# Level tables of a pre-LN attention and experts kernel: from 32 small loads per head to whole tables kept in memory

## Chip, cores and metric

The kernel runs on one core of one Trainium2 chip. The metric is the device time of one execution in microseconds (us). The engines are TensorE (PE, with its weight loads as PEld), VectorE (DVE), ScalarE (ACT), GpSimd (POOL) and SyncE (SP). SP computes nothing: it waits for semaphores and issues transfers, in the order of its program.

## The reference, cut to what matters

Eight sequences of 1024 tokens with 128 channels pass a layer of attention with a decay and a layer of eight experts of which two are used. In the attention a score is multiplied by a decay and by a weight that depends on the level of the distance between query and key (level 0 for distance 0, level l for a distance from 2^(l-1) up to 2^l):

```python
b, t, _ = x.shape                                   # 8, 1024, 128; H = 8 heads, LV = 12 levels
q = (x @ Wq.T).reshape(b, t, H, S); k = ...; v = ...
g = -jax.nn.softplus(x @ Wg.T + bg)
lam = jax.nn.softplus((x @ Wdl.T).reshape(b, t, H, LV) + Lparam)
G = jnp.cumsum(g, axis=1)
scores = jnp.einsum('bthd,bshd->bhts', q, k) * scale
decay = exp(G[t] - G[s]) for s <= t, else 0
lamw[b, h, t, s] = lam[b, t, h, level(t - s)]
A = scores * decay * lamw
out = einsum(A, v) @ Wo.T + x, then layer norm, then a top-2 mixture of 8 experts
```

## The kernel before

The 64 pairs of sequence and head are numbered n = 8 b + h and are worked through in one pipeline. Keys and queries are cut into tiles of 128. Within a head the scores fall into 12 groups (`GROUPS`), and each engine runs through 48 places (four for each group) in an order written out by hand: tables such as `PE_MORE`, `DVE_MORE` and `ACT_MORE` say which further piece stands at which place of which head. While the scores of head n are made, PE makes the logarithms of the weights of head n + 1 (`unit`, matmuls of line 1549 into `l_ps`), and ACT turns them into weights (`exps`, line 846). The preparation of sequence b + 1 and the end of sequence b - 1 are spread over the eight heads of sequence b.

The level weights come to PE in three tables for each head: `ra` (levels 0 to 7 for the query's own key tile), `rc` (levels 1 to 8 for the tile before) and `rb` (levels 8 to 10 for tiles 2 and 4 back). They are the moving operand; the masks are the stationary one. A table has one row for each offset of a query in a block, level and part (high, low); all of a row is zero (or a fixed number) but the queries of that offset, so that the data lie on a diagonal. The tables have two buffers each, filled with their fixed numbers once at the start. For each head SP loads the diagonal pieces from a scratch in device memory: 8 transfers for `ra`, 8 for `rc` (line 458) and 16 for `rb` (line 471). In the buffers the offset is not the outer index, so that a row's piece lies in runs of eight numbers (16 bytes).

Levels 9 and 10 of the farther keys take another way: rows of `ef_scratch` are spread to all partitions, `far` (line 480) and `farther` (line 485). ACT takes the exponential of `farther` for head n + 1 at place 15 of head n (`farther_exps`, line 863). DVE multiplies the query by it at place 21 (`take_q`, line 1087), then takes the low part of the query (line 1091), which frees a bank of `aux`; PE uses the product much later, for head n + 1 (`state_values`, line 1628).

Once a sequence, at h = 4 in SP's loop, `store_el` stores the logarithms of the next sequence: it waits until DVE has written their low parts (which is at place 243 of the sequence, that is place 3 of head 5), and then issues five stores (lines 451, 452 and 476). Only behind it come, in SP's program, `load_next_farther(n + 2)`, that is `farther` for head 6, and the tables for head 7. The order of SP in one step of its loop is:

```python
if h == 4 and b + 1 < B:
    store_el(b + 1)
if n + 2 < NH:
    load_next_farther(n + 2)
if n + 3 < NH:
    load_levels(n + 3)
```

Of the kernel before, what the change touches and what calls it, by code (L numbers as in the profile page):

```python
# [20 lines left out]
P = 128  # L21
# [55 lines left out]
_at = 0  # L77
for _name, _n in (("ma0", NTA * P), ("ma1", NTA * P), ("mb2", NTB * P), ("mb4", NTB * P),
                  ("ident", P), ("tri", P), ("suf", P), ("first", E), ("off", TA)):
    CONST[_name] = (_at, _at + _n)  # L80
    _at += _n
NCONST = _at
NMASK = CONST["ident"][0]
NCST = NCONST


def constants():

    def level(d):
        return np.where(d <= 0, 0, np.floor(np.log2(np.maximum(d, 1))).astype(np.int64) + 1)  # L90

    out = np.zeros((P, NCONST), np.float32)
    row = np.arange(P)
    s = np.arange(P)[None, None, :]

    def put(name, a):
# [12 lines left out]
    col = np.arange(TA)[None, :]  # L109
    off = np.where(q_a[:, 0] > col, NEVER, np.where(col == TA - 1, PAIR - 2 * PAIR * low_part[:, 0], 0.0))  # L110
    put("off", off * at_zero[:, 0] * (q_a[:, 0] != col))
    put("ma1", level(P + t_a - s) == l_a + 1)
# [12 lines left out]

def program(nc, x, Wq, Wk, Wv, Wg, bg, Wdl, Lparam, Wo, ln_g, ln_b, fWg, fbg, fWe, fbe, masks, table, out):

    m_dram = nc.dram_tensor("m_scratch", [H, P, 2, P], F32, kind="Internal").ap()
    n_dram = nc.dram_tensor("n_scratch", [H // 2, P, 2, 2, P], F32, kind="Internal").ap()
    ea_dram = nc.dram_tensor("ea_scratch", [B, H * (LOW + 1), 2, T], F16, kind="Internal").ap()  # L130
    eb_dram = nc.dram_tensor("eb_scratch", [B, H * HIGH, 2, T], F16, kind="Internal").ap()
    ef_dram = nc.dram_tensor("ef_scratch", [B, HIGH * H + H, NF], F32, kind="Internal").ap()

    with ExitStack() as outer:
        def sb(name, shape, dt=F32):
            return outer.enter_context(nc.sbuf_tensor(name, shape, dt))

        cst = sb("cst", [P, NCST - NMASK])
        mask = sb("mask", [P, NMASK], F16)
# [12 lines left out]

        main_stage(nc, x, Wq, Wk, Wv, Wg, bg, Wdl, Lparam, Wo, ln_g, ln_b, fWg, fbg, fWe, fbe, masks, table, out,
                   m_dram, n_dram, ea_dram, eb_dram, ef_dram, cst, mask, m, c, rows,
                   wet_hi, wet_lo, fwg2, wcat)
# [117 lines left out]
def main_stage(nc, x, Wq, Wk, Wv, Wg, bg, Wdl, Lparam, Wo, ln_g, ln_b, fWg, fbg, fWe, fbe, masks, table, out,  # L273
               m_dram, n_dram, ea_dram, eb_dram, ef_dram, cst, mask, m, c, rows,
               wet_hi, wet_lo, fwg2, wcat):

    with ExitStack() as ctx:
# [12 lines left out]
        nt = sb("nt", [P, 2, 2, P], F32R)  # L290
        ra = [sb(f"ra{k}", [P, NTA, TA, NC], F16) for k in range(2)]
        rc = [sb(f"rc{k}", [P, NTA, TA, NC], F16) for k in range(2)]
        rb = [sb(f"rb{k}", [KB, NTB, TB, NC], F16) for k in range(2)]

# [104 lines left out]
        out_done = [sem(f"out_done{f}") for f in range(2)]  # L399
        RA_IN, RB_IN, EL = TA * 16, TB * 16, 5 * 16  # L400
        lng = rows[:, NLOG:NLOG + P]
# [52 lines left out]
        def load_low(eng, n, qs, tables, first, landed):  # L454
            b, h = divmod(n, H)
            at = h * (LOW + 1) + first
            for q in qs:
                eng.dma_start(tables[n % 2][q * 2 * LOW:(q + 1) * 2 * LOW, :, q, :],  # L458
                              ea_dram[b, at:at + LOW, :, q * T // TA:(q + 1) * T // TA]
                              .rearrange("l r (t i) -> (l r) t i", i=NC)).then_inc(landed[n % 2], 16)  # L460

        def load_ra(eng, n, qs):
# [5 lines left out]
        def load_rb(eng, n, qs):  # L468
            b, h = divmod(n, H)
            for q in qs:  # L470
                eng.dma_start(rb[n % 2][q * 2 * HIGH:(q + 1) * 2 * HIGH, :, q, :],  # L471
                              eb_dram[b, h * HIGH:(h + 1) * HIGH, :, q * T // TB:(q + 1) * T // TB]
                              .rearrange("l r (t i) -> (l r) t i", i=NC)).then_inc(rb_in[n % 2], 16)
# [68 lines left out]
        with nc.Block() as block:  # L542
            @block.sync
            def _(sp):
                def load_x(b):
                    if b:
                        sp.wait_ge(t["stored"], EL * b)
                    sp.dma_start(tx[:, :, :], x[b].rearrange("(i t) c -> t i c", i=NC)).then_inc(t["x_in"], 16)

                def store_el(b):  # L550
# [3 lines left out]
                    sp.wait_ge(t["el_far"], 2 * (b + 1))  # L554
                    for part in range(2):
                        store_el_part(sp, b, part)
                    store_el_far(sp, b)

                def load_levels(n):
                    if n >= 2:  # L560
                        sp.wait_ge(l_mm, NU * (n - 1))
                    sp.wait_ge(t["stored"], EL * (n // H + 1))
# [7 lines left out]
                def load_next_farther(n):  # L570
                    sp.wait_ge(cq_done, n - 1)
                    sp.wait_ge(t["stored"], EL * (n // H + 1))
                    load_farther(sp, n)

                def load_last_x():
                    sp.wait_ge(t["stored"], EL * B)
                    sp.wait_ge(e["xb"], 2 * (B - 1))
# [46 lines left out]
                sp.dma_start(per_head(we), fWe.rearrange("e o c -> o e c")).then_inc(s_we, 16)  # L624
                sp.dma_start(mask[:, :], masks).then_inc(mask_in, 16)
                sp.wait_ge(s_hi, 1)
# [30 lines left out]
                for n in range(NH):  # L657
# [31 lines left out]
            def _(pool):  # L689
# [121 lines left out]
                for k in range(2):  # L811
                    pool.tensor_copy(ra[k][:, :, :, :], c("off")[:, None, :, None].broadcast_to([P, NTA, TA, NC])).then_inc(zeroed, 1)
                pool.wait_ge(ready, 3)
# [19 lines left out]
            def _(act):  # L833
# [75 lines left out]
                def token_abs(b):  # L909
                    if b:  # L910
                        act.wait_ge(t["stored"], EL * b)
                    for f in range(2):
# [611 lines left out]
            def _(pe):  # L1524
# [5 lines left out]
                def unit(n, u):  # L1530
                    k = n % 2
                    if u == 0:
                        pe.wait_ge(ra_in[k], RA_IN * (n // 2 + 1))
                    if u == 1:
                        pe.wait_ge(rc_in[k], RA_IN * (n // 2 + 1))
                    if u == 2:
                        pe.wait_ge(rb_in[k], RB_IN * (n // 2 + 1))
                    if n:
# [14 lines left out]
                    for d, i0, cnt in UNITS[u]:  # L1553
                        l_bank = [l_region(n, u)[:, f, slot * HF:(slot + cnt) * HF].rearrange("p (c i) -> p c i", i=cnt)
                                  for f in range(2)]
                        if d <= 1:
                            for tb in range(NTA):
                                f, at = divmod(tb * TA, HF)
                                last = mm(f, l_bank[f][:, at:at + TA, :], m(f"ma{d}")[:, tb * P:(tb + 1) * P],
                                          (ra, rc)[d][k][:, tb, :, i0:i0 + cnt])  # L1560
                        if d in (2, 4):
                            for tb in range(NTB):
                                f, at = divmod(tb * TB, HF)
                                last = mm(f, l_bank[f][:, at:at + TB, :], m(f"mb{d}", KB)[:, tb * P:(tb + 1) * P],
                                          rb[k][:, tb, :, i0:i0 + cnt])
                        slot += cnt
# [332 lines left out]
```

## Time and profile before

| what | value |
|---|---|
| time, median of 3 runs | 1448.07 us (1447.06 to 1449.88) |
| profiled execution, its own time | 1450.03 us |
| its span in the trace | 1448.2 us |
| PE busy | 1319.1 us, 91% |
| ACT busy | 1113.0 us, 77% |
| DVE busy | 1088.8 us, 75% |
| POOL busy | 798.9 us, 55% |
| packets of transfers | 414492, of which 339336 under 512 B |

A share of busy time says which engine has most to do over the whole run; a wait says who was held, by whom, and for how long. Matmuls are pipelined, so a PE that is busy isn't one at its peak. The profiled execution took 1450.03 us, 1.96 us more than the median.

### The profile page before, as it was taken

To read this page: it belongs to the slowest core of one execution; us is meant where nothing else is said; L and a number is where in the kernel's file an instruction comes from. 1 tells how busy PE (TensorE), PEld (TensorE's weight loads), DVE (VectorE), ACT (ScalarE), POOL (GpSimd) and SP (SyncE) were. 2 spreads that over 40 slices of the span, in tenths; PEclk is the share of its full clock that TensorE was granted. 3 is DMA by queue.
4 is the path that set the end of the run, shared out by engine and by line. 5 is a ranking of instruction groups with operands and counts; after the bars stand their busy time and mean duration, and the time that the engine had idled before them with its cause. 6 is when DMAs were issued, how large, how long until landed. Compare 5 with 4: busy or idle time off the path is not lost.

```text
span 1448.2 us, 31450 instructions
## 1 busy us (share of the span) xinstructions
PE 1319.1 (91%) x10278; PEld 1147.7 (79%) x10278; DVE 1088.8 (75%) x2732; ACT 1113.0 (77%) x3270; POOL 798.9 (55%) x956
## 2 busy tenths in 40 slices
PE   4699899989989899889999899998999989989987
PEld 4488788878888788777888788887888878878874
DVE  4757767787867878678776888678786787768777
ACT  3589888887788778888788877888778876877742
POOL 2244458744585456843568354873458544584553
PEclk9899999999999999999999999999999999999998
DMA  5422233223332243222332223322333223322300
GB/s 175 109 43 49 42 67 71 39 42 57 57 70 43 40 75 54 45 48 42 71 71 48 41 37 72 70 36 42 57 56 71 44 44 60 58 57 29 66 8 15
DMA packets 414492, 80.37 MB, mean 55 GB/s; under 512 B 339336, under 2 KB 404090, under 8 KB 414202
## 3 DMA queue, kind: packets, MB, share of 16 engines
q1 hardware_dynamic: 410984, 77.85, 28.5%
q8 instruction: 83, 1.36, 0.4%
q10 hardware_dynamic: 3346, 0.51, 0.2%
q14 instruction: 79, 0.65, 0.2%
HBM read 67.64 MB, written 10.09 MB: 54 GB/s over the span
## 4 chain that ended last, share of the span: by engine, by line
PE 42%; DVE 16%; ACT 14%; POOL 12%; SPq 7%; issue 5%; DMA 4%; ACTq 0%; POOLq 0%; DVEq 0%
PE o_ps L1606 9%; ACT w_all L846 5%; POOL a_lo_all L694 4%; PE s_ps L1526 4%; PE aux L1526 4%; PE s_ps L1528 4%; PE s_ps L1527 4%; SPq L458 3%; PE l_ps L1549 3%; PE aux L1528 3%; PE aux L1527 3%; DMA late<-in_L_attn_x 3%; SPq L471 2%; DVE a_all L1152 2%; DVE late L1382 2%
## 5 line engine op out<-in xcount | busy, mean ns | idle before, releaser
L694 POOL TENSOR_TENSOR a_lo_all<-a_all,a_hi 128x256 fp32r<-128x256 f32 (+2 forms) x576 | 580.4, 1021 | 545.8 <-ACT a_hi L894 544.9
L1152 DVE TENSOR_TENSOR a_all<-s_ps,w_all 128x512 f32<-128x512 f32 (+3 forms) x768 | 365.0, 485 | 185.5 <-PE s_ps L1528 123.2
L894 ACT ACTIVATE a_hi<-a_all 128x256 fp32r<-128x256 f32 (+2 forms) x576 | 308.1, 543 | 198.5 <-DVE a_all L1152 196.9
L846 ACT ACTIVATE w_all<-l_ps,bias 128x128 f32<-128x128 f32 x1589 | 440.4, 394 | 17.4 <-PE l_ps L1549 15.8
L1606 PE MATMUL o_ps<-a_hi,v_all 128*128 128x256 f32 (+2 forms) x1152 | 407.9, 362 | 4.5 <-POOL a_lo_all L694 4.5
L1606 PEld LDWEIGHTS o_ps<-a_hi,v_all 128*128 128x128 f32 x1152 | 222.3, 193 | 21.5 <-issue 3.9
L1526 PE MATMUL s_ps<-q_hi,xt_hi 128*128 128x256 f32 (+2 forms) x576 | 217.1, 377 | 6.9 <-DVE a_all L1152 5.7
L1528 PE MATMUL s_ps<-q_hi,xt_lo 128*128 128x256 f32 (+2 forms) x576 | 198.3, 344 | 0.0
L1527 PE MATMUL s_ps<-q_lo,xt_hi 128*128 128x256 f32 (+2 forms) x576 | 198.3, 344 | 0.0
L1606 PE MATMUL o_ps<-a_lo_all,v_all 128*128 128x256 f32 (+2 forms) x576 | 196.4, 341 | 0.0
L1526 PEld LDWEIGHTS s_ps<-q_hi,xt_hi 128*128 128x128 f32 x576 | 112.0, 194 | 18.0 <-DVE a_all L1152 9.7
L1382 DVE SCALAR_TENSOR_TENSOR late<-aux,gl,late 128x128 f32<-128x128 f32 x392 | 110.9, 343 | 16.5 <-PE aux L1528 16.5
L1528 PEld LDWEIGHTS s_ps<-q_hi,xt_lo 128*128 128x128 f32 x576 | 111.3, 193 | 8.5
L1527 PEld LDWEIGHTS s_ps<-q_lo,xt_hi 128*128 128x128 f32 x576 | 112.3, 195 | 6.8
L1606 PEld LDWEIGHTS o_ps<-a_lo_all,v_all 128*128 128x128 f32 x576 | 112.1, 195 | 5.7
L1078 DVE CAST q_hi<-aux 128x512 fp32r<-128x512 f32 x128 | 88.1, 688 | 32.9 <-PE aux L1528 31.7
L1121 DVE TENSOR_TENSOR v_all<-aux,v_all 128x512 fp32r<-128x512 f32 x128 | 87.9, 686 | 25.5 <-ACT v_all L886 25.1
L1549 PEld LDWEIGHTS l_ps<-rb,mask 96*128 96x128 f16 x1016 | 43.6, 98 | 74.5 <-issue 70.4
L1526 PE MATMUL aux<-nt,xt_hi 128*128 128x256 f32 x256 | 78.2, 305 | 25.2 <-DVE v_all L1121 20.5
L857 ACT ACTIVATE w_all<-far,bias 128x128 f32<-128x128 f32 x320 | 99.8, 389 | 0.0
L1549 PE MATMUL l_ps<-rb,mask 96*128 96x64 f16 (+1 forms) x1016 | 59.4, 202 | 41.0 <-ACT w_all L846 37.1
L1091 DVE TENSOR_TENSOR q_lo<-aux,q_hi 128x512 fp32r<-128x512 f32 x128 | 88.5, 692 | 4.4
(260 smaller groups left out, 2673.2 us busy)
## 6 DMA issues: line engine op xcount, KB each, us to landing
far<-ef_scratch SPq DMA_DIRECT2D x64, 320.0 KB, 3.6
rb<-eb_scratch SPq DMA_DIRECT2D x1016, 0.8 KB
farther<-ef_scratch SPq DMA_DIRECT2D x64, 192.0 KB, 3.4
ra<-ea_scratch SPq DMA_DIRECT2D x508, 4.0 KB, 2.2
rc<-ea_scratch SPq DMA_DIRECT2D x508, 4.0 KB, 2.0
mt<-m_scratch SPq DMA_DIRECT2D x62, 128.0 KB, 3.5
nt<-n_scratch SPq DMA_DIRECT2D x62, 128.0 KB, 3.4
tx<-in_L_attn_x SPq DMA_DIRECT2D x9, 512.0 KB, 5.6
```

The costliest lines, as they stand in the source:

```text
L694: pool.tensor_tensor(a_lo[r][:, 0:t1 - t0], a[r][:, 0:t1 - t0], a_hi[r][:, 0:t1 - t0].bitcast(F32), ALU.subtract).then_inc(a_lo_done, 1)
L846: last = act.activation(w[k][:, W_AT[j] + d, :].rearrange("p (f c) -> p f c", f=2), l_tiles[:, :, :, i - i0], ACT.Exp, bias=bias[b % 2][:, ...
L857: last = act.activation(w[k][:, W_AT[j] + FAR0, :], far[k][:, j * P:(j + 1) * P], ACT.Exp, bias=bias[b % 2][:, h, BIAS_AT[FAR0] + j:BIAS_A ...
L894: act.activation(a_hi[r][:, 0:t1 - t0], a[r][:, 0:t1 - t0], ACT.Copy).then_inc(a_hi_done, 1)
L1091: dve.tensor_tensor(q_lo[n % 2][:, cols], bank(piece), q_hi[n % 2][:, cols].bitcast(F32), ALU.subtract).then_inc(freed(piece), 1)
L1152: dve.tensor_tensor(a[(n * NG + g) % NA][:, 0:t1 - t0], s_ps[:, g % 2, 0:t1 - t0], w[n % 2][:, at:at + (t1 - t0) // P, :].rearrange("p i n ...
L1382: ins = dve.scalar_tensor_tensor(acc[:, i, :], bank(piece)[:, k * P:(k + 1) * P], gl[0][:, i, ex:ex + 1], acc[:, i, :], ALU.mult, ALU.add)
L1526: pe.matmul(o, a_hi, hi, start=True, stop=False)
L1527: pe.matmul(o, a_hi, lo, start=False, stop=False)
L1528: return pe.matmul(o, a_lo, hi, start=False, stop=True)
L1549: r = pe.matmul(o, lhsT, rhs, start=not started[f], stop=True, skip_group_check=True)
L1606: last = pe.matmul(o, lhs[:, vr, j, :], rhs[r][:, 0:t1 - t0], start=fresh, stop=True, skip_group_check=True)
```

## The change

From the second sequence on, whole tables stand in device memory for each head (`pa_scratch`, `pc_scratch`, `pb_scratch`, two sets for odd and even sequences). Their fixed numbers are copied there from a constant, for two heads in each step of SP's loop in the first four heads of the first and of the second sequence (`pad_tables`, three transfers per head, from device memory to device memory). `store_el` puts the diagonal pieces into these tables: for each head and part three transfers, 48 in all, in place of four stores of the whole logarithms (`store_tables`). A head of the second sequence or later is loaded by three transfers of whole tables (`load_tables`). The first sequence keeps the old way of loading. In the buffers the offset becomes the outer index, so that the piece of a row is one run (256 or 128 bytes), and a matmul reads its columns from 8 or 16 such runs. Waits on counts of transfers are adapted.

```diff
+        def stored_upto(b):
+
+            return EL + EL_MORE * (b - 1) if b else 0
...
+        def pad_tables(eng, b, h):
+            for dram, rows_, name in ((pa_dram, P, "pad_a"), (pc_dram, P, "pad_0"), (pb_dram, KB, "pad_0")):
+                eng.dma_start(dram[b % 2, h, 0:rows_ * T].rearrange("(r x) -> r x", x=T),
+                              masks[0:rows_, CONST[name][0]:CONST[name][1]]).then_inc(padded, 16)
+
+        def store_tables(eng, b, h):
+            for part, src in enumerate((elt_hi, elt_lo)):
+                for dram, r0, n_l, q in ((pa_dram, h * (LOW + 1), LOW, TA), (pc_dram, h * (LOW + 1) + 1, LOW, TA),
+                                         (pb_dram, NB_AT + h * HIGH, HIGH, TB)):
+                    to = dram[b % 2, h].rearrange("(q x) -> q x", q=q)[:, 0:2 * n_l * T].rearrange(
+                        "q (l r y) -> l r q y", l=n_l, r=2)[:, part, :, 0:T // q]
+                    eng.dma_start(to, src[r0:r0 + n_l, :].rearrange("l (q y) -> l q y", q=q)).then_inc(t["stored"], 16)
+
+        def load_tables(eng, n):
+            b, h = divmod(n, H)
+            for dram, rows_, to, landed in ((pa_dram, P, ra, ra_in), (pc_dram, P, rc, rc_in), (pb_dram, KB, rb, rb_in)):
+                eng.dma_start(to[n % 2][:, :, :, :].rearrange("p q t i -> p (q t i)"),
+                              dram[b % 2, h, 0:rows_ * T].rearrange("(r x) -> r x", x=T)).then_inc(landed[n % 2], 16)
...
-                    for part in range(2):
-                        store_el_part(sp, b, part)
+                    sp.wait_ge(padded, PADS * min(b, 2))
                     store_el_far(sp, b)
+                    for h in range(H):
+                        store_tables(sp, b, h)
...
-                    load_ra(sp, n, range(TA))
-                    load_rc(sp, n, range(TA))
-                    load_rb(sp, n, range(TB))
+                    if n < H:
+                        load_ra(sp, n, range(TA))
+                        load_rc(sp, n, range(TA))
+                        load_rb(sp, n, range(TB))
+                    else:
+                        load_tables(sp, n)
...
+                    if b < 2 and h < H // 2:
+                        for k in range(2):
+                            pad_tables(sp, b + 1, 2 * h + k)
...
-                                          (ra, rc)[d][k][:, tb, :, i0:i0 + cnt])
+                                          (ra, rc)[d][k][:, :, tb, i0:i0 + cnt])
...
-                                          rb[k][:, tb, :, i0:i0 + cnt])
+                                          rb[k][:, :, tb, i0:i0 + cnt])
```

Only SP's program gets other instructions; on PE, DVE, ACT and POOL the same instructions stand in the same order. The first place is SP around the store for the next sequence, in the first sequence (the later ones are like it). Before:

```order
L589 DMA mt<-m_scratch 128x256
L451 DMA ea_scratch<-tx 72x1024
L452 DMA eb_scratch<-tx 24x1024
L451 DMA ea_scratch<-tx 72x1024
L452 DMA eb_scratch<-tx 24x1024
L476 DMA ef_scratch<-lz 32x640
L485 DMA farther<-ef_scratch 128x384
L458 DMA ra<-ea_scratch 16x16x8 x8
L458 DMA rc<-ea_scratch 16x16x8 x8
L471 DMA rb<-eb_scratch 6x8x8 x16
```

In the changed kernel the same place reads as follows; the six rows of line 491 stand for one head, and stand eight times in all:

```order
L630 DMA mt<-m_scratch 128x256
L513 DMA ef_scratch<-lz 32x640
L491 DMA pa_scratch<-tx 8x8x128
L491 DMA pc_scratch<-tx 8x8x128
L491 DMA pb_scratch<-tx 3x16x64
L491 DMA pa_scratch<-tx 8x8x128
L491 DMA pc_scratch<-tx 8x8x128
L491 DMA pb_scratch<-tx 3x16x64
...
L522 DMA farther<-ef_scratch 128x384
L467 DMA ra<-ea_scratch 16x128 x8
```

Between the wait for DVE and the load of `farther` for head 6 there were 5 transfers, and there are now 49.

The second place is SP's step for a head from the second sequence on, `load_levels` in its midst. Before:

```order
L589 DMA mt<-m_scratch 128x256
L485 DMA farther<-ef_scratch 128x384
L458 DMA ra<-ea_scratch 16x16x8 x8
L458 DMA rc<-ea_scratch 16x16x8 x8
L471 DMA rb<-eb_scratch 6x8x8 x16
L480 DMA far<-ef_scratch 128x640
```

In the changed kernel, with the six transfers of `pad_tables` ahead of it, as it stands in the first four heads of the second sequence:

```order
L482 DMA pa_scratch<-in_masks 128x1024
L482 DMA pc_scratch<-in_masks 128x1024
L482 DMA pb_scratch<-in_masks 96x1024
L482 DMA pa_scratch<-in_masks 128x1024
L482 DMA pc_scratch<-in_masks 128x1024
L482 DMA pb_scratch<-in_masks 96x1024
L630 DMA mt<-m_scratch 128x256
L522 DMA farther<-ef_scratch 128x384
L496 DMA ra<-pa_scratch 128x1024
L496 DMA rc<-pc_scratch 128x1024
L496 DMA rb<-pb_scratch 96x1024
L517 DMA far<-ef_scratch 128x640
```

The 32 transfers of a head have become three, and six more stand ahead of `mt` and `farther` in eight steps of the loop.

## Rows read from the trace of the kernel before

**Rows 1.** Windows of three sequences: start:end, length, busy us (count) per engine, clock.

```profile
405.00:576.70 171.70, 160.90 (x1265) 140.84 (x1265) 132.63 (x331) 138.39 (x407) 99.13 (x121) 0.97 0.30 54
576.70:749.25 172.55, 160.53 (x1273) 140.71 (x1272) 134.04 (x335) 138.88 (x408) 99.95 (x122) 0.98 0.30 54
```

**Rows 2.** Waits ended by a transfer, and what follows: us in total, times, longest.

```profile
POOL late L735 <- DMA late<-in_L_attn_x: 23.0, 7, 4.2
...
ACT farther L863 <- DMA farther<-ef_scratch: 9.0, 7, 5.0
...
PE o_ps L1606 <- POOL a_lo_all L694: 4.5, 7, 1.9
...
PE l_ps L1549 <- DMA rb<-eb_scratch: 3.8, 1, 3.8
```

**Rows 3.** Waits of SP's queue, whole run.

```profile
SPq L485 <- PE o_ps L1628: 143.6, 32, 7.9
SPq L553 <- DVE tx L1252: 105.0, 7, 15.8
```

**Rows 4.** Timeline of SP in head 5 of the third sequence: start, us, what.

```profile
504.20 0.33 SPq L451 DMA_DIRECT2D ea_scratch<-tx  x1
...
505.81 0.35 SPq L476 DMA_DIRECT2D ef_scratch<-lz  x1
506.25 0.37 SPq L485 DMA_DIRECT2D farther<-ef_scratch  x1
506.72 3.87 SPq L458 DMA_DIRECT2D ra<-ea_scratch  x8
...
514.56 5.58 SPq L471 DMA_DIRECT2D rb<-eb_scratch  x16
```

**Rows 5.** Timeline of ACT, same place; idle time before it and its releaser in brackets.

```profile
507.43 1.94 ACT L846 ACTIVATE w_all<-l_ps,bias 128x128 f32<-128x128 f32 x7
509.89 0.53 ACT L863 ACTIVATE farther<-farther 128x384 f32<-128x384 f32 x1 [0.52 <-DMA farther<-ef_scratch]
```

**Rows 6.** The chain that ended last, 509.67 to 512.6: start, us, what.

```profile
510.40 0.42 DVE q_full L1082
510.82 0.47 DVE farther L1087
...
511.32 0.70 DVE q_lo L1091
...
512.07 0.50 PE aux L1526
```

**Rows 7.** DVE at the same place of the fifth sequence.

```profile
854.61 0.56 DVE L1087 TENSOR_TENSOR farther<-aux,farther 128x384 f32<-128x384 f32 x1 [0.40 <-ACT farther L863]
```

**Rows 8.** Tile `rb`, its loads: issue ns min/median/max, first and last start.

```profile
L471 SPq DMA_DIRECT2D rb<-eb_scratch x1016: 258/306/1289, 44.4 to 1361.5; - x170
```

**Rows 9.** Windows at the start, as rows 1 (last three numbers: clock, transfers, GB/s).

```profile
62.00:64.00 2.00, 1.21 (x21) 1.24 (x21) 2.00 (x10) 1.91 (x8) 0.86 (x1) 0.89 0.70 193
...
66.00:68.00 2.00, 0.00 (x0) 0.00 (x0) 0.00 (x0) 0.00 (x0) 1.76 (x2) 0.50 0.07 2
68.00:70.00 2.00, 1.85 (x12) 1.85 (x13) 0.00 (x0) 0.00 (x0) 1.00 (x3) 0.50 0.64 211
...
72.00:74.00 2.00, 2.00 (x14) 1.59 (x13) 0.74 (x2) 1.80 (x6) 0.91 (x2) 0.55 0.32 22
```

**Rows 10.** The page, transfers by issue: KB each, median us to landing; queue totals.

```profile
q1 hardware_dynamic: 410984, 77.85, 28.5%
...
farther<-ef_scratch SPq DMA_DIRECT2D x64, 192.0 KB, 3.4
...
mask<-in_masks SPq DMA_DIRECT2D x1, 1536.0 KB, 10.3
```

**Rows 11.** Groups by form: matmuls that read the tables, busy us, mean ns.

```profile
L1549 PE MATMUL l_ps<-ra,mask 128*128 128x64 f16 x1024 | 43.6, 198 | 0.0
...
L1549 PE MATMUL l_ps<-rb,mask 96*128 96x64 f16 x504 | 26.3, 195 | 0.0
```

More of the change, by code:

```diff
@@ L77 @@
 _at = 0
-for _name, _n in (("ma0", NTA * P), ("ma1", NTA * P), ("mb2", NTB * P), ("mb4", NTB * P),
+for _name, _n in (("ma0", NTA * P), ("ma1", NTA * P), ("mb2", NTB * P), ("mb4", NTB * P), ("pad_a", T), ("pad_0", T),
                   ("ident", P), ("tri", P), ("suf", P), ("first", E), ("off", TA)):
@@ L83 @@
 NMASK = CONST["ident"][0]
+NHELD = CONST["pad_a"][0]
+LEN_A = TA * (2 * LOW * T + T // TA)
+LEN_B = TB * (2 * HIGH * T + T // TB)
 NCST = NCONST
@@ L111, in constants @@
     put("off", off * at_zero[:, 0] * (q_a[:, 0] != col))
+    pad = off * at_zero[:, 0] * (q_a[:, 0] != col)
+    put("pad_a", np.broadcast_to(pad[:, :, None, None], (P, TA, NTA, NC)))
     put("ma1", level(P + t_a - s) == l_a + 1)
@@ L131, in program @@
     eb_dram = nc.dram_tensor("eb_scratch", [B, H * HIGH, 2, T], F16, kind="Internal").ap()
+    pa_dram, pc_dram = (nc.dram_tensor(n, [2, H, LEN_A], F16, kind="Internal").ap() for n in ("pa_scratch", "pc_scratch"))
+    pb_dram = nc.dram_tensor("pb_scratch", [2, H, LEN_B], F16, kind="Internal").ap()
     ef_dram = nc.dram_tensor("ef_scratch", [B, HIGH * H + H, NF], F32, kind="Internal").ap()
@@ L138, in program @@
         cst = sb("cst", [P, NCST - NMASK])
-        mask = sb("mask", [P, NMASK], F16)
+        mask = sb("mask", [P, NHELD], F16)
         rows = sb("rows", [P, NLOG + 2 * P + E])
@@ L153, in program @@
         main_stage(nc, x, Wq, Wk, Wv, Wg, bg, Wdl, Lparam, Wo, ln_g, ln_b, fWg, fbg, fWe, fbe, masks, table, out,
-                   m_dram, n_dram, ea_dram, eb_dram, ef_dram, cst, mask, m, c, rows,
+                   m_dram, n_dram, ea_dram, eb_dram, pa_dram, pc_dram, pb_dram, ef_dram, cst, mask, m, c, rows,
                    wet_hi, wet_lo, fwg2, wcat)
@@ L273, in main_stage @@
 def main_stage(nc, x, Wq, Wk, Wv, Wg, bg, Wdl, Lparam, Wo, ln_g, ln_b, fWg, fbg, fWe, fbe, masks, table, out,
-               m_dram, n_dram, ea_dram, eb_dram, ef_dram, cst, mask, m, c, rows,
+               m_dram, n_dram, ea_dram, eb_dram, pa_dram, pc_dram, pb_dram, ef_dram, cst, mask, m, c, rows,
                wet_hi, wet_lo, fwg2, wcat):
@@ L290, in main_stage @@
         nt = sb("nt", [P, 2, 2, P], F32R)
-        ra = [sb(f"ra{k}", [P, NTA, TA, NC], F16) for k in range(2)]
-        rc = [sb(f"rc{k}", [P, NTA, TA, NC], F16) for k in range(2)]
-        rb = [sb(f"rb{k}", [KB, NTB, TB, NC], F16) for k in range(2)]
+        ra = [sb(f"ra{k}", [P, TA, NTA, NC], F16) for k in range(2)]
+        rc = [sb(f"rc{k}", [P, TA, NTA, NC], F16) for k in range(2)]
+        rb = [sb(f"rb{k}", [KB, TB, NTB, NC], F16) for k in range(2)]
         far = [sb(f"far{k}", [P, NF]) for k in range(2)]
@@ L399, in main_stage @@
         out_done = [sem(f"out_done{f}") for f in range(2)]
-        RA_IN, RB_IN, EL = TA * 16, TB * 16, 5 * 16
+        EL, EL_MORE = 5 * 16, (6 * H + 1) * 16
+        PADS = 3 * H * 16
+        padded = sem("padded")
         lng = rows[:, NLOG:NLOG + P]
@@ L457, in load_low, with tables_in @@
             for q in qs:
-                eng.dma_start(tables[n % 2][q * 2 * LOW:(q + 1) * 2 * LOW, :, q, :],
+                eng.dma_start(tables[n % 2][q * 2 * LOW:(q + 1) * 2 * LOW, q, :, :],
                               ea_dram[b, at:at + LOW, :, q * T // TA:(q + 1) * T // TA]
                               .rearrange("l r (t i) -> (l r) t i", i=NC)).then_inc(landed[n % 2], 16)
+        def stored_upto(b):
+            return EL + EL_MORE * (b - 1) if b else 0
+        def tables_in(n, first):
+            k = n // 2 + 1
+            return 16 * (first * min(k, H // 2) + max(k - H // 2, 0))
+        def pad_tables(eng, b, h):
[14 more added lines that the diff above has]
+                              dram[b % 2, h, 0:rows_ * T].rearrange("(r x) -> r x", x=T)).then_inc(landed[n % 2], 16)
         def load_ra(eng, n, qs):
@@ L624, in _ @@
                 sp.dma_start(per_head(we), fWe.rearrange("e o c -> o e c")).then_inc(s_we, 16)
-                sp.dma_start(mask[:, :], masks).then_inc(mask_in, 16)
+                sp.dma_start(mask[:, :], masks[:, 0:NHELD]).then_inc(mask_in, 16)
                 sp.wait_ge(s_hi, 1)
@@ L1532, in unit @@
                     if u == 0:
-                        pe.wait_ge(ra_in[k], RA_IN * (n // 2 + 1))
+                        pe.wait_ge(ra_in[k], tables_in(n, TA))
                     if u == 1:
-                        pe.wait_ge(rc_in[k], RA_IN * (n // 2 + 1))
+                        pe.wait_ge(rc_in[k], tables_in(n, TA))
                     if u == 2:
-                        pe.wait_ge(rb_in[k], RB_IN * (n // 2 + 1))
+                        pe.wait_ge(rb_in[k], tables_in(n, TB))
                     if n:
```

14 lines of the change are left out of this document (7 added, 7 removed).

## The prediction

> **What bounds the kernel now.** I looked first at the engines by stretches. In a sequence in mid run PE is busy 160.9 of 171.7 us, and 160.5 of 172.6 in the next [rows 1]: some 11 us are idle in each, and ACT and DVE have 33 to 40. PE is the bound, and whatever stops it for longer than a few us is paid in full, since there is little idle time to make it up in. The second view was the waits that a transfer ends, since the change is about transfers. They are few [rows 2]: POOL waits 23.0 us in seven times for the residual, ACT 9.0 us in seven times for `farther`, PE 3.8 us once at the start for `rb`. No engine waits for `ra`, `rc` or, after the start, for `rb`. So the 32 loads that go away are hidden already, and what they can give back is bounded by these waits: 35.8 us in all, and on PE itself far less. The third view was SP's own waits [rows 3]: it waits 143.6 us for PE before it loads `farther` and 105.0 us for DVE before the store, 15 us each of seven times. SP has time to spare in most steps, but not at the store: it stands there until DVE is done, and what stands behind the store is wanted soon.
>
> That place I followed through the third sequence. The first store is issued at 504.20, the fifth at 505.81, `farther` for head 6 at 506.25 [rows 4]. ACT has finished its exponentials at 509.37 and sits idle until 509.89 for this very load [rows 5]. Its result is there at 510.42 and goes to DVE; the chain that ended last runs from 510.82 through DVE's `farther` and `q_lo` straight to PE at 512.07, which needs the bank that `q_lo` frees [rows 6]. So a `farther` that lands more than 0.40 us later moves PE. In the fifth sequence there is no slack at all, DVE itself waits for ACT [rows 7]. The load behind the store is on the path, seven times in a run.
>
> **The change part by part.** *The 48 stores.* Five transfers from the first store to `farther` took 2.05 us, 0.41 us apiece with the gap [rows 4]. Now 49 stand there. What one takes is not shown by the trace: it is a store from SBUF like those five, with 64 or 48 pieces. From below I take the loads of `rb`, of 48 pieces, 16 in 5.58 us, 0.349 apiece; from above those of `ra`, 256 pieces, 8 in 3.87, 0.484 [rows 4]. The likely value is that of the stores, the same direction and the same source tile: 0.41. Then `farther` is issued 49 x 0.41 = 20.1 us after the first store instead of 2.05, 18.0 us later (15.0 with 0.349, 21.7 with 0.484). Behind SP's late issue stands ACT at place 15, which is in order: the exponentials of places 22 and 30, the high parts of the scores, and the high parts of the values all wait. DVE stops at place 21 in `take_q`, and PE some three places later. Off goes the slack, 0.4 us in the sequence shown and none in others, on average 0.25. Seven times (18.0 - 0.25) is 124.3 us.
>
> What is next behind the store, the tables of head 7, `tx` and the tables of head 8, is late by as much, but head 6 starts late by the same, and three transfers replace 32 from the second sequence on, so I see no second stall there.
>
> *The clock after such a stall.* PE has one comparable stop, at the start: little work from 62 on, none from 66 to 68; the granted clock falls from 1.00 to 0.50 within the window 62 to 64 and is still at 0.50 when PE starts again at 68.15, with PE busy nearly all the time; in the window 72 to 74 the mean is 0.55, so it rose at 73.8 [rows 9]. That is 1.2 GHz instead of 2.4 for 5.6 us of full work, which costs 2.8 us. The new stops are longer, so I take 2.8 for each; 0 is the lower end, if ACT and DVE hold PE after the restart. Seven times 2.8 is 19.6.
>
> *The 32 loads that become three.* They cost SP 3.87 us for `ra`, as much for `rc` and 5.58 for `rb`, some 13.4 us a head with the gaps [rows 4], and now about 1.2. What waits for SP because of them is the residual: POOL's 23.0 us. POOL has idle time and PE waits for POOL only 4.5 us in seven times [rows 2]. Between 0 and 23 I take the row on PE, -4 us. ACT's remaining waits for `farther` are part of the store above. At the start the loads of `ra` and `rc` shrink from 256 pieces to 16: 24 of them stand ahead of the `rb` load that PE waits 3.8 us for, and at `rb`'s issue time each saves 0.135 us, 3.2 together. I take -3.
>
> *The pads.* Six transfers in eight steps, 704 KB a head read and written again. A step moves 1408 KB; the one row near it, 1536 KB of masks, took 10.3 us [rows 10], so about 9.4 us of queue ahead of the next `farther` and `mt`. In the second sequence SP is early and most of it is over by the time something is wanted; in the first two or three heads SP has no lead, and one or two loads can be late by 3 to 6 us. From 0 to 10, taken as +5.
>
> *Whole tables instead of diagonals.* 704 KB a head instead of 76, but in rows of 2 KB; `farther` with 192 KB lands in 3.4 us [rows 10], and the tables are wanted a head later. Cost 0, hidden behind the 20 us of a head; with that cover gone it would be some 10 us a head.
>
> *Matmuls that read short runs.* The 16 bytes of a block are now 256 bytes from the next. The nearest row is the `rb` matmul that reads four of every eight numbers: 195 ns, against 198 for 64 numbers in a row [rows 11]. So 0. The upper end is a read at half the rate: 43.6 us for 1024 matmuls [rows 11] is 0.043 each, and twice that for the 48 of each of 64 heads adds 131 us in all; I see no sign of it.
>
> **The sum** goes against the profiled execution, 1450.0: +124.3 +19.6 -4 -3 +5 = +141.9, or 1592. The median of the runs lies 1.96 us under that execution, so the predicted time is 1590 us.
>
> **A rule weighed.** The queue's packets took 28.5% of 16 engines' span, 410984 of them [rows 10]: 16 ns each on average, small ones for the most part. A store of 48 or 64 pieces that spreads over 16 engines would keep each of them for under 0.1 us, far less than its issue, so that the issue sets the pace of the sum above. The Trainium skill speaks against such a spread ("DMA: Bandwidth & Descriptors", section "Why a DMA increments its semaphore by 16 and not by 1"): a transfer runs on the largest number of engines, up to 16, that divides the outer dimensions of both sides, which here would be 8 engines for a `pa` or `pc` store and 3 for a `pb` store, always the lowest. No row shows which engines a store uses. By the page three engines would get 512 pieces in a sequence, an estimate of 8.2 us at 16 ns, and the sum would stay; at over 39 ns a piece it would grow, and that is the second rival.
>
> **Rivals.** *The delay is partly made up* (12%). PE has 11 us idle in a sequence [rows 1]; if all of it closed up behind the stall, the cost is 18.0 + 2.8 - 0.25 - 10.8 = 9.8 each, and the time about 1515. For it: ACT and DVE have a quarter of their time free. Against it: they stop too and can work nothing ahead.
>
> *The stores queue up behind each other* (10%). Small pieces to device memory may take longer than they are issued. Take 0.67 us a store, 1.4 times what a load of `ra` with its 256 pieces takes to issue [rows 4]: 49 of them last 32.8 us instead of 20.1, `farther` lands another 12.7 us late, and the time is 1590 + 89 = about 1680. For it: nothing in the trace shows such short stores. Against it: the packets' mean, and loads of `ra` with four times the pieces, which go out every 0.484 us.
>
> *The matmuls slow down* (4%): at half the rate 1590 + 131 = about 1720.
>
> *Not slower* (8%): the store's issue is short. If a store were issued in 0.10 us, `farther` would be 49 x 0.10 - 2.05 - 0.25 = 2.6 us late, 18 in all, and all the waits for transfers, 35.8 us, would go if every one reached the end: about 1430. It decides at 0.15 us a store. The shortest issue of any `rb` load is 0.258 us [rows 8], so that I give it little.
>
> **How the numbers follow.** The forecast has 66%, its own range is 1550 to 1625 (issue of 0.35 to 0.48 us, clock 0 to 2.8, pads 0 to 10). The range from 1520 to 1650 takes in most of the first rival and the lighter half of the second, and leaves out about 2 in 10. Chances: faster by more than 0.2% (about what a measurement of this kernel can tell) 5%, within it 2%, slower 93%.
>
> **What would show it.** In the profile after: SP's timeline with 48 short stores of about 0.41 us in a row, seven times, and `farther` some 20 us behind the first; ACT's wait for `farther` about 18 us each, some 125 in all instead of 9.0; PE idle for 15 us and more at this place, with the clock at 0.50 behind it; no wait for `ra`, `rc`, `rb`; POOL's wait for the residual mostly gone; line 1549's matmuls still near 195 ns. Wrong I would be if `farther` were issued as early as before or ACT did not wait there.

## The result, and the profile after

The changed kernel takes **1558.65 us**, the median of 4 runs (1556.89 to 1561.34), beside 1448.97 us (1447.06 to 1450.19, 4 runs) for the kernel before in the same session: 1.0766 times as long, 95% interval 1.0742 to 1.0791. The forecast was 1590 us. The profiled execution took 1556.89 us with a span of 1555.1 us, 106.9 us more than that of before; the clock granted on average fell from 0.970 to 0.944.

First the view in which the change can be looked for: the waits that a transfer ends, and what follows from them, over the whole run (us in total, times, longest).

```profile
DVE farther L1131 <- ACT farther L907: 124.7, 21, 15.7
ACT farther L907 <- DMA farther<-ef_scratch: 121.1, 11, 16.6
...
PE aux L1570 <- DVE q_lo L1135: 92.4, 6, 15.8
...
POOL late L779 <- DMA late<-in_L_attn_x: 10.2, 7, 2.0
```

The rows read as a chain: PE waits for DVE's `q_lo`, DVE for ACT's `farther`, ACT for the load of `farther`. ACT's wait was 9.0 us in [rows 2] and is now 121.1. POOL's wait for the residual has shrunk from 23.0 to 10.2, and no wait for the tables of a later sequence is in the view. PE's row counts six stalls; in the seventh, that of the first sequence, its wait stands in another row, `PE l_ps L1593 <- ACT w_all L890: 51.2, 46, 13.0`, whose longest is that stall.

Then SP at the store, third sequence (start, us, what), the place of [rows 4]:

```profile
533.99 0.32 SPq L513 DMA_DIRECT2D ef_scratch<-lz  x1
534.35 0.33 SPq L491 DMA_DIRECT2D pa_scratch<-tx  x1
...
550.85 0.29 SPq L491 DMA_DIRECT2D pb_scratch<-tx  x1
551.24 0.34 SPq L522 DMA_DIRECT2D farther<-ef_scratch  x1
```

From the first store to `farther` 17.25 us pass, with 49 transfers: 0.352 us apiece. Before it was 2.05 us. So `farther` goes out 15.2 us later, where 18.0 were forecast.

What that does to the engines stands in the chain that ended last, from 550.85 on (start, us, what):

```profile
550.85 0.29 SPq L491
...
551.24 4.11 DMA farther<-ef_scratch
...
555.37 0.53 ACT farther L907
...
555.92 0.57 DVE farther L1131
...
556.52 0.70 DVE q_lo L1135
...
557.26 0.79 PE aux L1570
```

It is the chain of [rows 6] with SP's stores and the transfer put ahead of it. The transfer itself takes 4.1 us from its issue, hardly longer than the 3.64 us of before (issued 506.25 [rows 4], used 509.89 [rows 5]): it stands in no queue behind the stores. ACT's row at 555.37 says how long it had stood, PE's at 557.26 likewise:

```profile
555.37 0.52 ACT L907 ACTIVATE farther<-farther 128x384 f32<-128x384 f32 x1 [16.22 <-DMA farther<-ef_scratch]
```

```profile
557.26 0.79 PE L1570 MATMUL aux<-wet_hi,x2t 128*128 128x512 f32 x1 [15.47 <-DVE q_lo L1135]
```

The same stretch in windows (busy us and count for PE, PE's loads, DVE, ACT, POOL; clock, busy share of the 16 DMA engines, GB/s):

```profile
536.00:540.00 4.00, 3.97 (x44) 3.41 (x44) 3.48 (x11) 3.15 (x12) 1.18 (x2) 1.00 0.25 36
540.00:544.00 4.00, 1.79 (x11) 1.32 (x10) 0.57 (x2) 0.00 (x0) 0.00 (x0) 1.00 0.28 38
544.00:548.00 4.00, 0.00 (x0) 0.00 (x0) 0.00 (x0) 0.00 (x0) 0.00 (x0) 0.69 0.28 39
548.00:552.00 4.00, 0.00 (x0) 0.00 (x0) 0.00 (x0) 0.00 (x0) 0.00 (x0) 0.50 0.27 37
...
556.00:560.00 4.00, 2.74 (x7) 2.16 (x8) 1.64 (x3) 3.50 (x12) 1.74 (x2) 0.50 1.02 268
560.00:562.00 2.00, 2.00 (x14) 1.60 (x13) 1.29 (x2) 0.99 (x3) 0.34 (x1) 0.50 0.00 1
562.00:564.00 2.00, 2.00 (x14) 1.87 (x13) 1.03 (x3) 1.13 (x5) 0.94 (x1) 0.85 0.04 8
```

All four compute engines stand still from 542 to 552, while SP issues. The clock falls to half in the stall, is at 0.50 when PE starts again at 557.26, and the mean of 0.85 in the window from 562 puts its rise at 562.6 (0.5 for 0.6 us and 1.0 for 1.4): 5.3 us at 1.2 GHz instead of 2.4 in this stall.

To see where the 106.9 us lie, I compared the start of the state matmuls (line 1628 before, 1672 after) head by head in the two traces. The shift between them grows in head 5 of each sequence but the last, and hardly elsewhere:

```
sequence                            1      2      3      4      5      6      7     sum
head 5, added us                 14.79  17.51  17.72  17.49  17.75  16.39  16.86   118.5
head 1 of the first sequence, added                                                 +4.6
first head                                                                          -1.7
all other heads, together                                                          -14.5
shift at the last head                                                            +106.9
```

Last, the matmuls that read the tables, by form, as [rows 11] (busy us, mean ns), and the page's line for the queue:

```profile
L1593 PE MATMUL l_ps<-ra,mask 128*128 128x64 f16 x1024 | 42.7, 197 | 0.0
...
L1593 PE MATMUL l_ps<-rb,mask 96*128 96x64 f16 x504 | 27.5, 198 | 13.0 <-ACT w_all L890 13.0
```

```profile
q1 hardware_dynamic: 134008, 126.95, 29.5%
```

Matmuls that read 16-byte blocks 256 bytes apart cost what they did before (198 and 195 ns). The 13.0 us of idle time in the second row are the stall of the first sequence. The queue moves 1.6 times the megabytes in a third of the packets and is hardly busier (28.5% before [rows 10]).

### The profile page after: what moved, and what is told of

Its sections match the earlier page's. It is cut to its first block, busy times and chain, and to the rows that moved or that the text cites. A ratio compares the mean times of both kernels' runs of the same rounds, so it can differ in the third digit from the quotient of the medians.

```text
span 1555.1 us, 30182 instructions
## 1 busy us (share of the span) xinstructions
PE 1327.2 (85%) x10278; PEld 1153.0 (74%) x10278; DVE 1087.7 (70%) x2732; ACT 1113.1 (72%) x3270; POOL 799.0 (51%) x956
## 4 chain that ended last, share of the span: by engine, by line
PE 43%; DVE 16%; ACT 16%; SPq 11%; POOL 6%; issue 5%; DMA 3%; ACTq 0%; POOLq 0%; DVEq 0%
PE o_ps L1650 9%; SPq L491 7%; ACT w_all L890 6%; PE s_ps L1570 5%; PE s_ps L1571 4%; PE s_ps L1572 4%; PE aux L1570 3%; PE l_ps L1593 3%; PE aux L1572 3%; PE aux L1571 3%; DVE a_all L1196 2%; POOL a_lo_all L738 2%; DMA farther<-ef_scratch 2%; ACT a_hi L938 2%; DVE late L1426 2%
## 5 line engine op out<-in xcount | busy, mean ns | idle before, releaser
L890 ACT ACTIVATE w_all<-l_ps,bias 128x128 f32<-128x128 f32 x1589 | 439.9, 392 | 14.9 <-PE l_ps L1593 6.7
L1570 PE MATMUL aux<-wet_hi,x2t 128*128 128x512 f32 x116 | 54.1, 467 | 100.2 <-DVE q_lo L1135 92.4
L907 ACT ACTIVATE farther<-farther 128x384 f32<-128x384 f32 x64 | 37.2, 581 | 121.1 <-DMA farther<-ef_scratch 121.1
L1131 DVE TENSOR_TENSOR farther<-aux,farther 128x384 f32<-128x384 f32 x62 | 34.1, 550 | 124.7 <-ACT farther L907 124.7
L1593 PEld LDWEIGHTS l_ps<-rb,mask 96*128 96x128 f16 x1016 | 44.3, 99 | 82.9 <-issue 66.8
L1570 PEld LDWEIGHTS aux<-wet_hi,x2t 128*128 128x128 f32 x116 | 22.5, 194 | 106.9 <-DVE q_lo L1135 95.3
```

What stands on the lines that cost most here:

```text
L890: last = act.activation(w[k][:, W_AT[j] + d, :].rearrange("p (f c) -> p f c", f=2), l_tiles[:, :, :, i - i0], ACT.Exp, bias=bias[b % 2][:, ...
L1570: pe.matmul(o, a_hi, hi, start=True, stop=False)
L1593: r = pe.matmul(o, lhsT, rhs, start=not started[f], stop=True, skip_group_check=True)
```

## The experiments

Theory A: 48 stores in a row on SP's queue hold back the load of `farther` behind them by their issue time alone, and ACT, DVE and PE stand for it. Theory B, its rival: the stores are slow in the DMA engines, so that what comes behind them lands late wherever it is issued. Beside these stood the smaller terms: the clock, the new layout, the pads. The first four kernels ran beside the kernel before at 1448.02 us (22 runs, 1441.79 to 1454.76), the other four beside it at 1448.74 us (15 runs, 1443.23 to 1453.68).

**1. `farther` ahead of the stores.** Changed kernel, SP's step: the load moves past the block of stores, nothing else.

```diff
-                    if h == 4 and b + 1 < B:
-                        store_el(b + 1)
                     if n + 2 < NH:
                         load_next_farther(n + 2)
+                    if h == 4 and b + 1 < B:
+                        store_el(b + 1)
```

> The changed kernel with one edit: in SP's step the load of `farther` stands ahead of the store, so that 49 stores no longer stand before it. Theory A (the 110 us are the late issue of `farther` behind the stores, seven times): the seven waits of ACT go from about 16 us each to under 1, and head 5 of each sequence takes about as long as in the kernel before. The tables of head 7 still stand behind the stores and should land some 3 us after PE wants them, which leaves up to 20 us: 1440 to 1465 us. Theory B (the stores disturb the queues, so that whatever is loaded beside them is late): ACT still waits 10 us or more, and the time stays above 1520.

Measured: 1461.27 us (1460.76 to 1467.44, 4 runs), ratio 1.0093 [1.0067, 1.0119]. Waits:

```profile
ACT farther L907 <- DMA farther<-ef_scratch: 20.0, 7, 6.3
...
PE l_ps L1593 <- DMA ra<-pa_scratch: 6.1, 6, 1.4
...
PE l_ps L1593 <- DMA ra<-ea_scratch: 4.8, 1, 4.8
```

The stores are all still there, and 97 of the 110 us are gone (1558.65 - 1461.27), so the order is the cause. That alone doesn't tell theory A from theory B, since `farther` now passes the stores altogether: in the third sequence it is issued at 508.63, and the stores begin at 515.69. What stands behind them tells: `ra` goes out at 532.88, right behind the last store, and the matmul that waits for it starts at 535.69, 2.8 us later.

```profile
535.69 0.64 PE L1593 MATMUL l_ps<-ra,mask 128*128 128x64 f16 x16 [0.98 <-DMA ra<-pa_scratch]
```

A load behind 48 stores lands soon after its own issue, as `farther` did in the changed kernel (4.1 us). Theory A holds, and theory B doesn't. What is late next is the tables: `ra` waits for its turn behind the stores, and PE waits for it in head 6, 14.5 us added in the first sequence, where 32 loads stand there and more than the tables is late, and 1.1 to 4.8 us in the others, where there are three.

**2. Both loads ahead of the stores.** The tables' loads too.

```diff
-                    if h == 4 and b + 1 < B:
-                        store_el(b + 1)
                     if n + 2 < NH:
                         load_next_farther(n + 2)
                     if n + 3 < NH:
                         load_levels(n + 3)
+                    if h == 4 and b + 1 < B:
+                        store_el(b + 1)
```

> The changed kernel with `farther` for head 6 and the tables for head 7 both loaded ahead of the store. Theory A: no engine waits behind the stores any more, and what is left of the change is the rest of its sum: head 1 of the first sequence about 5 us longer (pads), the start about 2 us shorter, and about 1.5 us a sequence less waiting for the residual. That gives 1448 + 5 - 2 - 11 = 1440 us, between 1435 and 1450. Theory B: above 1500.

Measured: 1444.38 us (1434.83 to 1452.69, 12 runs), ratio 0.9961 [0.9937, 0.9986]. The waits for `ra` are gone. Two losses remain, both in the first sequence: 6 us in head 1 and 11.4 us in head 6. SP's rows there show the second (start, us, what):

```profile
179.38 0.31 SPq L513 DMA_DIRECT2D ef_scratch<-lz  x1
...
197.86 0.41 SPq L585 DMA_DIRECT2D tx<-in_L_attn_x  x1
...
199.00 0.37 SPq L522 DMA_DIRECT2D farther<-ef_scratch  x1
```

The next step's `farther`, for head 7, stands behind all the stores and behind `tx`. ACT waits 9.3 us for it. In later sequences SP is early enough for this.

**3. The new layout alone.** The kernel before, with the order of the buffers' dimensions as in the changed kernel, and the same 32 loads a head and five stores.

```diff
-        ra = [sb(f"ra{k}", [P, NTA, TA, NC], F16) for k in range(2)]
+        ra = [sb(f"ra{k}", [P, TA, NTA, NC], F16) for k in range(2)]
...
-                eng.dma_start(tables[n % 2][q * 2 * LOW:(q + 1) * 2 * LOW, :, q, :],
+                eng.dma_start(tables[n % 2][q * 2 * LOW:(q + 1) * 2 * LOW, q, :, :],
...
-                                          (ra, rc)[d][k][:, tb, :, i0:i0 + cnt])
+                                          (ra, rc)[d][k][:, :, tb, i0:i0 + cnt])
```

> The kernel before with the buffers' new layout alone (offset outermost, one run for each piece, matmuls that read runs of 8 numbers 256 or 128 bytes apart), no whole tables, no pads, no new stores. If matmuls don't mind the runs, line 1549's groups stay at 194 to 208 ns, the issue of `ra` and `rc` falls from 0.448 to 0.420 us, and the time is 1442 to 1449 us. If they slow down, each of the groups gets longer by 10 ns or more and the time is above 1470.

Measured: 1441.75 us (1438.79 to 1446.7, 11 runs), ratio 0.9958 [0.994, 0.9976]. Matmuls by form, then waits and the page's queue line:

```profile
L1549 PE MATMUL l_ps<-ra,mask 128*128 128x64 f16 x1024 | 43.6, 198 | 0.0
...
L1549 PE MATMUL l_ps<-rb,mask 96*128 96x64 f16 x504 | 26.4, 194 | 0.0
```

```profile
POOL late L735 <- DMA late<-in_L_attn_x: 18.6, 7, 3.4
...
ACT farther L863 <- DMA farther<-ef_scratch: 3.8, 6, 2.3
```

```profile
q1 hardware_dynamic: 124472, 77.85, 19.6%
```

SP's issue of `ra` in the kernel before, then here (ns, min/median/max):

```profile
L458 SPq DMA_DIRECT2D ra<-ea_scratch x508: 302/448/1764, 40.3 to 1351.7; - x170
L458 SPq DMA_DIRECT2D ra<-ea_scratch x508: 303/420/1837, 40.9 to 1340.6; - x170
```

The matmuls are unchanged, and yet the kernel gains 0.4%, a quarter of a microsecond more than the range expected. The packets changed most: the same 77.85 MB in 124472 packets instead of 410984, and 19.6% of the engines' span instead of 28.5% [rows 10]. The 8.9% are some 2100 us of 16 engines' time, over 286512 packets 7 ns for each one saved. The Trainium skill states a fixed overhead of each packet in "DMA: Bandwidth & Descriptors", section "Why small descriptors are slow (HBM only)"; the direction agrees, 28.5% to 19.6%.

That the packets made the kernel faster is not shown, since two more things changed with them. A load of `ra` or `rc` is issued in 0.420 us instead of 0.448. And the granted clock was higher, 0.974 against 0.970 in the profiled executions: added up over its spells at 1.2 GHz between the first and the last head, PE works 39 us at that level instead of 55, and half of that difference, an estimate of 7.7 us, is most of the 10.5 us that this execution is shorter. Why the clock fell less often stays open.

**4. The clock kept up.** Changed kernel, 65 matmuls into an unused bank while PE waits for DVE in head 5, in the second to seventh sequence; they add work that nothing reads.

```diff
+                        if n % H == 5 and place == 25 and n // H + 1 < B and n > H:
+                            pe.wait_ge(a_done, n * NG + 6)
+                            keep_busy(s_ps[:, 1, :], 65)
```

> The changed kernel with 65 further matmuls of the masks into a free bank at place 25 of head 5, in six of the seven sequences with a store: some 14 us of work for PE in each stall, whose results nobody uses. If the drop of the clock costs about 2.2 us in each stall, the granted clock stays at 1.0 through it, and the time falls by 10 to 14 us to about 1545 to 1549. If PE is held by ACT and DVE after the restart anyway, the time stays at 1558.

Measured: 1546.8 us (1545.69 to 1547.84, 4 runs), ratio 1.0676 [1.0648, 1.0703]. A window inside the stall, then PE's rows of the third sequence:

```profile
542.00:546.00 4.00, 4.00 (x21) 1.77 (x19) 0.00 (x0) 0.00 (x0) 0.00 (x0) 1.00 0.28 38
```

```profile
539.08 14.20 PE L1854 MATMUL s_ps<-mask 128*128 128x512 f16 x65
...
554.34 0.50 PE L1570 MATMUL aux<-wet_hi,x2t 128*128 128x512 f32 x1 [1.06 <-DVE q_lo L1135]
```

ACT still waits 15.85 us for `farther`, but the clock stays at 1.00 and the matmul behind the stall takes 0.50 us instead of 0.79. The median is 11.9 us under the changed kernel's, and the six head 5 lose 13.7 us less: 2.0 to 2.3 us a stall are the clock's, where the prediction took 2.8.

**5. Half the stores.** Changed kernel, only the 24 transfers of the high parts; the low parts of the logarithms are left out of the tables from the second sequence on (the count of transfers that is waited for follows).

```diff
-            for part, src in enumerate((elt_hi, elt_lo)):
+            for part, src in ((0, elt_hi),):
```

> The changed kernel with the 24 stores of the high parts alone; the low parts of the level weights' logarithms are left out from the second sequence on. If the price is the issue of the stores one after the other, 0.345 us each, `farther` comes 24 x 0.345 = 8.3 us earlier, ACT's wait is some 7.5 us instead of 16, and the time is 1558 - 58 = 1500 us, some 10 less if the clock no longer falls. If the price were something fixed for each store phase (the drain of the queue, the receipts), the waits would stay above 12 us.

Measured: 1500.26 us (1497.54 to 1501.73, 4 runs), ratio 1.0353 [1.0328, 1.0377]. SP's rows in the third sequence:

```profile
518.35 0.32 SPq L513 DMA_DIRECT2D ef_scratch<-lz  x1
...
527.03 0.34 SPq L522 DMA_DIRECT2D farther<-ef_scratch  x1
```

8.68 us for 25 transfers, 0.347 each, and ACT's waits 62.6 us instead of 121.1. Half the stores are half the loss (51.5 of 109.7 us), so the loss grows with their number and is not a fixed price of having such a batch. They are also half the pieces and half the bytes; whether a transfer of other pieces would cost the same this run doesn't tell.

**6. The pads behind the loads.** As experiment 2, with the pads moved behind the step's loads too.

```diff
-                    if b < 2 and h < H // 2:
-                        for k in range(2):
-                            pad_tables(sp, b + 1, 2 * h + k)
...
                         load_levels(n + 3)
+                    if b < 2 and h < H // 2:
+                        for k in range(2):
+                            pad_tables(sp, b + 1, 2 * h + k)
```

> `farther` and the tables ahead of the store, and the six pads of a step behind its loads instead of ahead of `mt` and `farther`. If the pads are what makes head 1 of the first sequence 6 us longer, the second state_values comes some 2 us before that of the kernel before instead of 3.9 after it, and the time is 1438 us, 1432 to 1443. If they only move the wait elsewhere: 1444.

Measured: 1442.83 us (1438.86 to 1446.67, 7 runs), ratio 0.9953 [0.9934, 0.9972]; 1438 was expected. The loss in head 1 is gone, but one of 5.9 us stands in head 3 of the first sequence, where `nt` is now behind the pads:

```profile
PE aux L1570 <- DMA nt<-n_scratch: 4.1, 1, 4.1
```

**7. The stores in two halves.** As experiment 6, with the tables of heads 0 to 3 stored behind the loads of one step and those of heads 4 to 7 behind `farther` of the next, and the load of `tx` behind these.

```diff
-                    for h in range(H):
+                    for h in range(H // 2):
                         store_tables(sp, b, h)
...
                         load_next_farther(n + 2)
+                    if h == 5 and b + 1 < B:
+                        for k in range(H // 2, H):
+                            store_tables(sp, b + 1, k)
+                    if h == 5 and b + 2 < B:
+                        load_x(b + 2)
```

> As the one before, and the store of the tables in two halves: heads 0 to 3 behind the loads of SP's step 4, heads 4 to 7 behind `farther` of step 5, with the load of `tx` behind them. If the 11 us that head 6 of the first sequence still loses are `farther` for head 7, which stood behind all 48 stores and `tx`, they go, and the time is some 1428 us, 1422 to 1435, below both kernels. If the wait has another cause, the time stays at 1438.

Measured: 1436.19 us (1428.9 to 1436.93, 6 runs), ratio 0.990 [0.9874, 0.9925], the fastest of all. What is left of the waits:

```profile
PE aux L1573 <- DMA nt<-n_scratch: 5.2, 2, 4.3
...
ACT farther L910 <- DMA farther<-ef_scratch: 3.7, 1, 3.7
```

Head 6 of the first sequence no longer loses anything. It came out above the expected 1428, and above the range of 1422 to 1435: the loss in head 3 stayed (6.0 us), and of the 10.7 us that head 6 lost in experiment 6 only 6.8 arrive at the last head.

**8. Layout alone, `farther` ahead of the five stores.** Experiment 3 with the order of experiment 1.

> The kernel before with the new layout of the buffers and with `farther` ahead of its five stores, without tables, pads or new stores. The waits of ACT for `farther` in heads 5, some 0.6 us each, go: 1442 - 4 = 1438 us. If they were slack it stays at 1442.

Measured: 1442.46 us (1436.91 to 1443.38, 7 runs), ratio 0.9954 [0.9934, 0.9975], the same as experiment 3. ACT's waits at the store are gone from the trace, and the time doesn't move. The 0.6 us each of the expectation were those of the kernel before; with the new layout alone they had already shrunk to some 0.3 (3.8 us in all, 2.3 of them at the start), no more than the slack behind them. Experiment 7 has the dense loads and the short stores beside this layout, and is 6.3 us faster, with intervals of the ratio that do not overlap. What of that comes from the loads and what from its other order was not told apart.

## Why the prediction was right in its steps and high in its size

**What held.** The sign, the place and the chain: seven stalls, one in each sequence, at the load behind the store, through ACT and DVE to PE. Experiment 1 shows it by taking only the order away. The range and the likeliest case's own range held the time.

**The issue of a store** is the term that was mis-sized. I took 0.41 us, that of the five large stores; a short one took 0.352 with the gap in the third sequence, and 0.345 to 0.361 on average in each of the seven. That is about the lower bound, the loads of `rb` with as many pieces, 0.349. So those loads were the nearer likeness, not the stores with the same direction and source; what in a transfer sets its issue is not shown, since the old stores of 24 rows took 0.37 with fewer pieces. In the third sequence the delay is 15.2 us, 0.5 more for the landing and 0.4 less for the slack, 15.3 in all; with the clock's 2.3 that makes 17.6, and 17.72 were measured. Over the seven heads 118.5 us less the clock's 16.1 leaves 102.4, where the term said 124.3. The first sequence's stall is the shortest, 14.8: before the change ACT did not wait for `farther` there, so that more slack came off.

**The clock** was there, and PE was busy at 1.2 GHz behind the restart (2.74 us of the window that ends 2.74 us after it). But I took the 5.6 us of the one stop at the start for every stall. The third has 5.3, and the seven go from 3.4 to 5.8; the longest and the shortest, the fifth and the sixth, in windows (PE starts at 932.28 and 1119.01):

```profile
932.00:934.00 2.00, 1.72 (x4) 1.45 (x5) 0.69 (x2) 2.00 (x8) 0.69 (x2) 0.50 1.13 292
...
936.00:938.00 2.00, 2.00 (x13) 1.71 (x13) 0.53 (x1) 1.74 (x5) 1.29 (x1) 0.50 0.00 0
938.00:940.00 2.00, 2.00 (x16) 1.87 (x15) 1.80 (x6) 0.63 (x1) 0.47 (x1) 0.98 0.00 0
...
1119.00:1121.00 2.00, 1.99 (x5) 1.61 (x6) 0.42 (x1) 2.00 (x7) 0.95 (x1) 0.50 1.14 300
1121.00:1123.00 2.00, 2.00 (x15) 1.64 (x14) 1.03 (x2) 0.55 (x2) 0.06 (x1) 0.65 0.25 64
```

The clock rises 5.8 us after the restart in the fifth and 3.4 in the sixth. Over the seven stalls these spells add up to 32.3 us, half of which is 16.1, or 2.3 a stall; experiment 4 gives 2.0 to 2.3, some 14 to 16 in all instead of 19.6.

**The residual and the other waits** were mis-sized the other way: -4 forecast, -14.5 measured in all heads beside the stalls and pads. The 32 loads that became three are not shown to be the cause: experiment 3 keeps them, and its final shift is already -10.5 us in the profiled execution (-6.3 in the median). Some half of it is the clock elsewhere, which I had not counted: in these other heads PE works 51 us at 1.2 GHz in the trace of before and 36 in that of the changed kernel, and half of the difference is again an estimate of 7.7 us. Head 2 of the eighth sequence, which has no store, shows it. It is 1.8 us shorter; the kernel before comes first:

```profile
1282.20:1306.10 23.90, 20.10 (x149) 17.66 (x148) 14.68 (x35) 15.96 (x48) 21.92 (x31) 0.86 0.24 48
1390.80:1412.90 22.10, 17.77 (x148) 15.35 (x148) 14.76 (x35) 15.84 (x48) 20.45 (x30) 1.00 0.26 75
```

Executions of one kernel differ in the same way: the twelve of experiment 2 go from 1434.83 us at a clock of 0.982 to 1452.69 at 0.965. What makes the clock fall less often in the changed kernel, the layout, the loads or chance, stays open.

**Pads and start** were nearly right: +4.6 against +5 and -1.7 against -3. **Whole tables** cost nothing that the trace shows, and **short runs** cost PE nothing (197 and 198 ns).

In one line: 102.4 + 16.1 + 4.6 - 1.7 - 14.5 = 106.9, against 124.3 + 19.6 + 5 - 3 - 4 = 141.9.

**The rivals.** *Partly made up*: no, the shift of head 5 stays through the heads behind it. What was smaller was the stall itself. *Queue up*: no, `farther` lands 4.1 us after its issue behind 48 stores, and half the stores are half the loss. The packets in the trace say the same: the last of the 48 packets of each `pb` store in the third sequence starts 1.0 to 1.4 us after the store's issue, the sixteenth store's like the first's. That bears on the rule that I weighed. The Trainium skill would have 8 engines take a `pa` or `pc` store and 3 a `pb` store ("DMA: Bandwidth & Descriptors", section "Why a DMA increments its semaphore by 16 and not by 1"). The trace names no engine, but its count of packets agrees: beside the data lie 320 packets of four bytes in the train of each sequence and 168 in that of experiment 5, which is 16 for `ef_scratch` and 8, 8 and 3 for each three stores, if every engine that takes part writes one. The estimate by that rule wanted over 39 ns a packet for a backlog; a packet of a `pb` store took 13 ns and one of a `pa` or `pc` store 27. *Matmuls slow*: no. *Not slower*: no, a store would have had to be issued within 0.15 us, and the shortest of the 336 took 0.264.

## What to carry to other kernels

A transfer on an in-order queue costs its issue, here about 0.35 us with the gap for stores of 6 and 16 KB; before cutting one transfer into many, count them and look at what stands behind the batch and how soon an engine wants it. Put the loads that are wanted next ahead of the batch, or cut the batch over two steps: the same 48 stores cost 7.7% in one order and went with a kernel 1% faster than the old one in another. When such a batch is moved, follow the next load behind it, since the wait may only move, as it did to the tables, to the next `farther` and to `nt`.

## What the runs showed of the hardware

Issue times by line (ns, min/median/max), two of the changed kernel and two of the kernel before:

```profile
L491 SPq DMA_DIRECT2D pb_scratch<-tx x112: 279/288/326, 168.3 to 1300.2; - x112
```

```profile
L482 SPq DMA_DIRECT2D pa_scratch<-in_masks x16: 496/595/987, 82.6 to 295.9; - x16
```

```profile
L451 SPq DMA_DIRECT2D ea_scratch<-tx x15: 332/350/391, 36.2 to 1191.6; - x15
L452 SPq DMA_DIRECT2D eb_scratch<-tx x15: 333/371/1063, 36.7 to 1192.0; - x15
```

A store of 48 pieces is issued in 0.29 us, less than one of 72 or 24 rows of 2 KB (0.35 and 0.37), and a copy of 128 such rows within device memory takes 0.60. The other surprise is the layout: runs of 256 bytes instead of 16 gave 0.4% with the instructions otherwise the same. The engines' share that they free, 28.5% to 19.6%, is the largest difference in that trace; that it is the cause is not shown.
